# Window attention with transposed scores made from masked keys alone, on one core

## The reference

```python
qkv = x @ in_w.T + in_b
q, k, v = heads of 8 channels
scores = einsum('nhid,nhjd->nhij', q, k) / sqrt(8)
attn = softmax(scores)
out = einsum('nhij,nhjd->nhid', attn, v) @ out_w.T + out_b
y = x + window_reverse(out @ proj_w.T + proj_b)
result = y + fc2(gelu(fc1(ln(y))))
```

## Time and profile before

| | |
|---|---|
| median of 3 runs | 88.28 us (87.34 to 88.77) |
| the profiled execution: span, first to last instruction | 86.4 us |
| around the span, to the median | 1.88 us |
| TensorE busy, matmul records | 79.8 us, 1578 |
| VectorE busy | 66.7 us |
| ScalarE, GpSimd busy | 51.1, 53.3 us |
| TensorE's granted clock, mean | 0.996 of full |

### The profile page before, as it was taken

The page is one execution under the profiler, slowest core; times in us unless marked ns, Lnnn a source line. Parts: engine busy times, 40 slices in busy tenths (PEclk is TensorE's granted clock), DMA queues, the critical chain, the costliest instruction groups (busy, mean ns, idle before and its releaser), DMA issues.

```text
span 86.4 us, 3871 instructions
## 1 busy us (share of the span) xinstructions
PE 79.8 (92%) x1578; PEld 46.1 (53%) x1578; DVE 66.7 (77%) x216; ACT 51.1 (59%) x85; POOL 53.3 (62%) x64
## 2 busy tenths in 40 slices
PE   5999999987999999899999989999999999999950
PEld 5988657444666665664666635554554423223420
DVE  4998998989989979989989987999762964333160
ACT  0296798976358836858578366354588556634400
POOL 7988828995593980899696596896908044800000
PEclk9999999999999999999999999999999999999998
DMA  0999510111010111111111202000000000031142
GB/s 19 206 337 441 231 38 0 34 61 52 31 52 31 46 53 49 53 46 38 46 52 39 66 17 67 31 8 0 8 0 0 0 8 0 0 121 68 53 156 91
DMA packets 3617, 5.72 MB, mean 66 GB/s; under 512 B 1072, under 2 KB 1840, under 8 KB 3472
## 3 DMA queue, kind: packets, MB, share of 16 engines
q1 hardware_dynamic: 2736, 3.08, 11.0%
q10 hardware_dynamic: 864, 2.40, 7.4%
HBM read 2.66 MB, written 1.05 MB: 43 GB/s over the span
## 4 chain that ended last, share of the span: by engine, by line
PE 66%; DVE 21%; issue 8%; ACT 1%; DVEq 0%; ACTq 0%
PE ps_s L323 12%; PE ps_u L414 8%; PE ps_t L275 6%; PE ps_u L484 5%; DVE row_max L644 4%; DVE stats L624 3%; PE ps_t L323 3%; PE ps_t L468 3%; PE ps_t L397 3%; PE ps_m L323 3%; PE ps_s L468 2%; PE ps_m L297 2%; PE ps_o L428 2%; PE ps_o L484 2%; DVE sums L663 2%
## 5 line engine op out<-in xcount | busy, mean ns | idle before, releaser
L1047 POOL TENSOR_TENSOR max_x<-max_t,early 128x512 bf16<-128x512 bf16 x14 | 14.7, 1047 | 9.7 <-DVE max_t L657 9.7
L644 DVE TENSOR_REDUCE row_max<-ps_s 128x16 f32<-128x1024 f32 x15 | 18.1, 1209 | 1.5 <-PE ps_s L323 1.2
L919 ACT ACTIVATE probs<-ps_t 128x1024 f32<-128x1024 f32 x13 | 13.3, 1024 | 8.9 <-PE ps_t L397 8.4
L323 PE MATMUL ps_s<-masked,qk 32*64 32x256 f32 x240 | 16.6, 387 | 1.6 <-DVE row_max L644 0.6
L323 PE MATMUL ps_t<-masked,qk 32*64 32x256 f32 x224 | 15.3, 387 | 0.0
L1056 POOL TENSOR_TENSOR rstd<-y_var,minus_half 128x4 f32<-128x4 f32 x8 | 8.3, 1034 | 6.9 <-DVE y_var L707 6.9
L323 PEld LDWEIGHTS ps_s<-masked,qk 32*64 32x64 f32 x240 | 7.9, 131 | 6.1 <-issue 2.4
L414 PE MATMUL ps_u<-probs,vz 128*32 128x64 f32 x512 | 10.6, 222 | 0.0
L414 PEld LDWEIGHTS ps_u<-probs,vz 128*32 128x32 f32 x512 | 8.0, 109 | 3.4 <-issue 3.0
L1032 POOL TENSOR_TENSOR rstd<-var,minus_half 128x4 f32<-128x4 f32 x8 | 8.6, 1076 | 1.0 <-DVE var L632 0.4
L275 PE MATMUL ps_t<-zeros 128*128 128x128 f32 x32 | 7.1, 389 | 1.0 <-DVE zeros L818 1.0
(11 more groups left out here) (114 smaller groups left out, 149.9 us busy)
## 6 DMA issues: line engine op xcount, KB each, us to landing
masked<-qk SPq DMA_DIRECT2D x54, 32.0 KB, 1.9
x_ch<-x_ch_d ACTq DMA_DIRECT2D x1, 1024.0 KB, 8.1
out_d<-result SPq DMA_DIRECT2D x3, 256.0 KB, 2.5
x_tok<-x_tok_d ACTq DMA_DIRECT2D x1, 512.0 KB, 6.1
late<-late_d ACTq DMA_DIRECT2D x1, 352.0 KB, 5.3
x_tok<-x_tok_d SPq DMA_DIRECT2D x2, 128.0 KB, 3.4
x_tok<-x_tok_d ACTq DMA_DIRECT2D x1, 256.0 KB, 4.9
out_d<-result SPq DMA_DIRECT2D x2, 128.0 KB, 2.3
```

Source lines behind the costliest of these rows:

```text
L323: return nc.tensor.matmul(ps[o:o + L, g, n * TOK:(n + 1) * TOK], qk[r:r + RG, b, w, t], masked[r:r + RG, b, :, w, t], start=(n == 0), stop ...
L644: nc.vector.tensor_reduce(row_max[:, w, 0:16], score_bank(k, w)[:].rearrange("q g (h j) -> q (g h) j", j=L), axis=AX.X, op=ALU.max).then_i ...
L919: nc.scalar.activation(probs[:, w, :], scores_t_bank(k, w)[:].rearrange("q g c -> q (g c)"), ACT.Exp).then_inc(probs_done, 1)
L1047: nc.gpsimd.tensor_tensor(max_x[:, k % 2, w, :].rearrange("q (n i) -> q n i", n=16), bf16_high(max_t[:, w, :]).unsqueeze(1).to_broadcast([ ...
```

## The change

The masked queries are gone. Masked keys serve both products: as moving operand of the straight scores, as before, and as stationary operand of the transposed ones, with the plain queries of one window moving. A stationary operand has 64 columns, one head of one window, so each transposed product of 256 columns becomes four of 64. In each tile both products now use the same rows of the array. So that the straight scores of tile `t+1` and the transposed ones of tile `t` still use different rows, tiles alternate: in even tiles queries (and masked keys) lie on partitions 0 to 63, in odd ones on 64 to 127. The mask buffers are halved, two tiles to a buffer. The bias and the query scale need a second column with the halves swapped, hence two more products and one more VectorE operation at the start. ScalarE's `mask_q_first`, VectorE's `mask_k_half(2)`, the memsets `zero_masked(2)` and `zero_masked(3)`, and 28 of 54 transfers go.

```diff
@@ addresses
+        def q_rows(k):
+            return C * (k % 2)
+        def k_rows(k):
+            return C - q_rows(k)
+        def masked_keys(k, h, w):
+            return masked[q_rows(k):q_rows(k) + C, k // 2 % 2, h, w]
@@ SyncE
-            mask_heads(0, C, 0, q_masked[0], 2)
             for k in range(1, TILES):
-                mask_heads(k, 0, C, k_masked[k % QB], 2 if k in (1, 2) else SLOTS)
-                mask_heads(k, C, 0, q_masked[k % QB])
+                mask_keys(k, 2 if k == 1 else SLOTS)
@@ TensorE
+            def score_t_unit(j, w, n, h, g, u):
+                r = q_rows(j) + RG * g
+                t = slice((2 * n + u) * L, (2 * n + u + 1) * L)
+                c = n * TOK + h * L
+                return nc.tensor.matmul(scores_t_bank(j, w)[L * u:L * u + L, g, c:c + L],
+                                        masked[r:r + RG, j // 2 % 2, h, w, t], qk[r:r + RG, j % QB, w, t],
+                                        start=(n == 0 and h == 0), stop=True,
+                                        skip_group_check=True, tile_position=(r, L * u))
...
             def scores_t_ready(k, w):
-                if w == 0:
-                    pe.wait_ge(q_masked[k % QB], 64 * (k // QB) + (64 if k % QB else 32))
-                if k == 0:
-                    pe.wait_ge(q_masked_act, w + 1)
...
+            def scores_t_block(j, w, n):
+                for h in range(SLOTS):
+                    for g in range(2):
+                        for u in range(2):
+                            score_t_unit(j, w, n, h, g, u)
             def scores_both(k, w, j, v):
...
                 for n in range(BLK):
                     for g in range(2):
                         for u in range(2):
-                            ins = score_unit(ps_s, 0, qk, k, w, n, g, u)
+                            ins = score_unit(k, w, n, g, u)
                     if n == BLK - 1:
                         ins.then_inc(scores_done, 1)
-                    for g in range(2):
-                        for u in range(2):
-                            score_unit(scores_t_bank(j, v), C, qk, j, v, n, g, u)
+                    scores_t_block(j, v, n)
...
+            nc.tensor.matmul(ps_o[0:C, 0, 1:2], w_in_t[0:C, C:2 * C], vec[0:C, B1:B1 + 1],
+                             start=True, stop=True)
+            nc.tensor.matmul(ps_o[C:P, 0, 1:2], w_in_t[0:C, 0:C], vec[0:C, B1:B1 + 1],
                              start=True, stop=True).then_inc(bias_product_done, 1)
@@ VectorE
-                if t == 0:
-                    mask_k_half(2)
...
+            for e in range(2):
+                nc.vector.tensor_scalar(b_qk[:, e:e + 1], ps_o[:, 0, e:e + 1], vec[:, BQK + e:BQK + e + 1],
+                                        vec[:, QS + e:QS + e + 1], op0=ALU.add, op1=ALU.mult).then_inc(b_qk_made, 1)
@@ ScalarE
-            mask_q_first(0)
             copy_xn(1)
-            mask_q_first(1)
@@ GpSimd
-            zero_masked(2)
...
-            pool.wait_ge(max_found, 1)
-            zero_masked(3)
```

More of the change, by code:

```diff
@@ L34 @@
 AHEAD = 3
[L35 to L36 removed]
+NV = 12
+B1, BQK, QS, BV, OUTB, PROJB, B2, FC2B, FC1B = 0, 1, 3, 5, 6, 7, 8, 9, 10
 E_VEC = 0
@@ L103, in swin_block_kernel @@
         qk = sb("qk", [P, QB, 2, TOK])
-        masked = sb("masked", [P, QB, SLOTS, 2, TOK])
+        masked = sb("masked", [P, QB // 2, SLOTS, 2, TOK])
         vz = sb("vz", [P, VB, 2, BLK, HEADS, 4 * D])
@@ L140, in swin_block_kernel @@
         mean_w_set = sem("mean_w_set")
-        masked_zeroed = [sem(f"masked_zeroed{i}") for i in range(QB)]
+        masked_zeroed = [sem(f"masked_zeroed{i}") for i in range(QB // 2)]
         vz_zeroed = sem("vz_zeroed")
@@ L247, in _, with mask_keys @@
         def _(sp):
-            def mask_heads(k, dst, src, done, heads=SLOTS):
-                b = k % QB
+            def mask_keys(k, heads=SLOTS):
                 sp.wait_ge(qk_copied, k + 1)
                 if k < QB:
-                    sp.wait_ge(masked_zeroed[k], 1)
+                    sp.wait_ge(masked_zeroed[k // 2], 1)
                 else:
@@ L316, in project_qkv, with score_unit @@
                 project_v(k)
-            def score_unit(ps, base, stationary, k, w, n, g, u):
-                b = k % QB
-                r = base + RG * g
+            def score_unit(k, w, n, g, u):
+                r = q_rows(k) + RG * g
                 t = slice((2 * n + u) * L, (2 * n + u + 1) * L)
-                o = L * (u if base else u ^ g)
-                return nc.tensor.matmul(ps[o:o + L, g, n * TOK:(n + 1) * TOK], qk[r:r + RG, b, w, t],
-                                        masked[r:r + RG, b, :, w, t], start=(n == 0), stop=True,
+                o = L * (u ^ g)
+                return nc.tensor.matmul(score_bank(k, w)[o:o + L, g, n * TOK:(n + 1) * TOK], qk[r:r + RG, k % QB, w, t],
+                                        masked[r:r + RG, k // 2 % 2, :, w, t], start=(n == 0), stop=True,
                                         skip_group_check=True, tile_position=(r, o))
+            def score_t_unit(j, w, n, h, g, u):
[6 more added lines that the diff above has]
+                                        skip_group_check=True, tile_position=(r, L * u))
             def scores_ready(k, w):
@@ L377, in scores_t @@
                 for n in range(BLK):
-                    for g in range(2):
-                        for u in range(2):
-                            score_unit(scores_t_bank(j, w), C, qk, j, w, n, g, u)
+                    scores_t_block(j, w, n)
             def shift_scores(k, w):
@@ L934, in mask_k_first @@
                 for w in range(2):
-                    nc.scalar.activation(masked[0:C, 0, 3, w], qk[C:P, 0, w], ACT.Copy,
+                    nc.scalar.activation(masked_keys(0, 3, w), qk[C:P, 0, w], ACT.Copy,
                                          scale=slot_mask[C:P, 3:4]).then_inc(k_masked_act, 1)
[L938 to L941, removed]
             def square_mean(k):
```

36 lines of the change are left out of this document (19 added, 17 removed).

## The result

The changed kernel takes **101.19 us** (median of four runs, 100.88 to 102.42) against 88.44: ratio 1.148, 95% interval 1.138 to 1.158. The forecast was 93.5, with a range up to 97.0. The direction was right, the size was not: +12.7 us instead of +5.2. The profiled execution has a span of 99.4 us, 13.0 more than before. Some executions of a kernel take a few per cent longer than others; from here on the time of an experiment is the median of its runs within 1.5% of the fastest, ratios go by these runs, and brackets hold the least and the greatest of all runs.

The account below looks back on a forecast made before the run. It took TensorE to bound the kernel nearly all the way from 21.04 us, VectorE before. Blocks 5.04, a wait taken up -0.3, lone transposed blocks +0.1 and start +0.4 gave 5.2 on 88.28: 93.5 us, range 88.8 to 97.

Parts of the forecast that it names:

- rival 3: TensorE's instruction queue: added instructions come too slowly, with stops per added packet; +2.7 us on the forecast, 96.2; chance 0.10.
- The mixed block: Straight and transposed scores together on TensorE: +0.42 us a block over 1.05, twelve blocks paying, 5.04 us.
- reach: TensorE in mixed blocks: looks 16 products ahead, counted from the oldest unfinished; by the working 0.46 us more a block.
- the second straight group: Sign in the mixed block: its records start near 0.66 us after the block and not at 0.48.
- The start, +0.4: Second bias column before the first mask: 0.2 us on TensorE and 0.2 on VectorE, with 0 and 0.6 as ends.
- The first masks on VectorE: Sign at the start: first masks at about 10.3 us, against 9.87 before, would confirm the start's price.
- the first mixed block: Tile 1's straight scores with tile 0's transposed ones, before 21.04 us with VectorE as the bound: costs nothing.
- What is removed, 0: Query masks, a VectorE mask half, memsets and transfers dropped: 0 gained, at most 1.6 us if their cover were gone.
- no tile's masks come later: Mask transfers: tile 2's two new ones stand where tile 1's query transfers stood, so no delay.
- Rival 1: Mixed blocks: the halves run freely, 0.06 us more a block, 1.2 us in all, 89.5; chance 0.24.
- Rival 4: Masks and transfers: their relief counts and all 1.6 us come back, 87.9 or 86.7; chance 0.08.
- Rival 2: Mixed blocks: strict order or no overlap, or halves taking turns by group at 0.76 a block, 97.6; chance 0.08.

Follow-up runs that it names:

- experiment 7: Kernel before, with products that nothing reads added behind its last one, in parts of 64, 128 and 256 columns; the first part took 11.9 us.
- experiment 5: Changed kernel with its straight score products in one bf16 pass; 96.99 us, ratio to before 1.100.
- experiment 2: Changed kernel with mixed blocks reordered: two heads of transposed products, four straight, three heads, four straight, three heads; 100.03 us, ratio to before 1.145.
- (3, one run): Changed kernel with all 8 straight products of a mixed block ahead of all 32 transposed ones; 99.81 us.
- (6): Changed kernel with its transposed score products in one bf16 pass, all 32 of a block kept; 89.1 us, ratio 1.013.
- experiment 9: Kernel before with the straight score products alone in one bf16 pass; four runs gave 88.02 to 93.04 us.

## Why the prediction was wrong

The step that failed is the delivery of instructions: the sum has no term for it, and rival 3, which stood for it, priced it at +2.7 us. The runs put most of the 12.7 us there. The parts follow one by one.

**The mixed block: the mechanism right, the size too small.** The changed kernel shows the hole: 33 records (16.5 products) are started, then none for 0.2 us until the first straight group is done. Reordering moved the block to 1.33 and to 1.86 as a reach of that size would. The Trainium skill, page "TensorE: Matmul & The Clock Gate", gives a queue of 64 instructions with partial reordering in the table at its head; 33 records with their loads, 66 instructions, agree. I predicted +0.42 (0.46 by the working); it was +0.63. The other 0.17 lies behind the holes: transposed records there start every 16.5 ns and not every 14.6, the fourth head's come before the second straight group (0.73 in place of 0.66), and the last head's take 0.15 in place of 0.06.

**"Instructions come too slowly": the step that failed.** It stood as rival 3 with a chance of 0.10 and +2.7 us. It held two errors. First the price: I took the 0.29 us of idle time for the cost of a stop. But that block of the kernel before took 1.97 us where its neighbours took 1.05, so the stop cost 0.92: behind it, what otherwise stands side by side went one after the other. Second the form: I counted stops per added packet, "one stop in 12 pieces", as if each were a matter of luck. It is a rate. From one stop's end to the next's, where 250 to 256 loads and products lie between them, no profile has less than 3.4 us, and the kernel before went at 4.5 in this stretch, with about a fifth in hand. The change adds 962 instructions to 1,572 there. By an estimate with experiment 7's 3.45 us for 256, the 2,534 need 34.1 us where 27.6 were taken: 6.5 us more in this stretch alone, from the counts, before any block is looked at. Measured were 9.7 more. The price per 256 was not on record before these runs; what the trace did show was the one stop, and that its block took 0.92 us longer.

The Trainium skill, page "Runtime: NRT & Kernel Launch", section "Instruction fetch mechanics", says that instructions come in blocks of 256 and that TensorE has room for 2,048. Experiment 7's 256 between two stops agrees with the first. A store of 2,048 that is used up before the first stop does not show: in the changed kernel the packets come one by one, 3.4 to 5.0 us apart, from 14 to 77 us, and experiment 5's first stop behind 22 us comes after 945 records. Why the changed kernel's first stop comes only at 40 us stays open. The page also holds that the fetch is hidden, because no engine issues faster than about 20 cycles an instruction; here the measurement decides: in tile 0's lone transposed block (15.91 to 17.00 us of the changed kernel) the records start 14.6 ns apart with a load to each, 7.3 ns an instruction, and the stops are the fetch no longer hidden.

**So the sum's terms don't add.** Blocks (+8.0) and stops (+5) look like two causes in the trace. Taking 7 us out of the blocks brought back 4.2, and this one had a packet of instructions fewer (experiment 5), 4.2 brought back 1.2 (2), lengthening them by 2 cost nothing (3, one run). With the instructions taken out, all but 1.1 of the 12.7 came back (6). From about 40 us on the block's length is covered by the delivery, and my whole argument on the reach prices something that is mostly hidden there.

**The start, +0.4:** the trace said +1.2, but the part that belongs to the change is 0.14 at the first scores; the rest differs from execution to execution. The first masks on VectorE, expected at 10.3 us, came at 10.7 in the changed kernel's profile and at 9.6 in experiment 2's. At the lone straight block (21.04 before, 22.24 after) two profiles with early fast steps, experiments 7 and 3, have 20.66 and 21.12. By this one pair 0.4 was about right, though its parts were not: the first mixed block, priced at nothing, lies in it.

**What is removed, 0:** as predicted, as far as these runs tell. Splitting alone, with all masks and transfers kept, took 99.67 (to 102.17) against 101.19; at one pass the changed kernel was not faster than the one before. The transfers are not always free: in experiment 7's profile, whose first 83 us are the kernel before, TensorE waited 1.3 us at 53.97 us for a mask transfer that took 3.6. And one clause was wrong: "no tile's masks come later". All four of tile 2's masks are now transfers; the last landed at 24.70 us in the changed kernel, just ahead of the block at 24.84, and in kernel 2, whose start was faster, TensorE waited 0.5 us for it (the row has also 0.3 us for tile 1's):
```profile
PE ps_t L336 <- DMA masked<-qk: 0.8, 2, 0.5
```

**The rivals.** Rival 1 (halves run freely, 0.24) fell with the first block: 0.73 and not 0.48. Rival 4 needed it. Rival 2's time of 97.6 was nearest to the measurement, but for a reason that is not there: nearness by luck. The right cause, rival 3, had a chance of 0.10 and a price a fifth of the loss.

## What to carry to other kernels

Count instructions before products: an fp32 product is two loads and two passes, and cutting 256 columns into four times 64 quadruples them at equal work. Divide each stage's instructions on the busiest queue by its time; in this kernel 256 in 4.5 us was nearly free (one stop) and 256 in 3.6 to 3.9 us was the wall, and at the wall shorter blocks gave back a fraction of what they saved. Price a stop by how much longer its surroundings take, not by its idle time.

## What the runs showed of the hardware

- TensorE's instructions arrived at no more than 256 in 3.45 us in a stream without waits or transfers (one interval, granted clock mostly 0.50), and 256 in 3.6 to 3.9 us in the attention stage at full clock. The shortest time from one stop's end to the next's in any profile was 3.38 us.
- They came in packets of 16 KB. 72 stops without a releaser ended 1.1 to 1.6 us after a packet had landed; in the changed kernel the next packet started 1.1 to 1.3 us after the stop's end.
- TensorE started instructions out of order up to 16.5 fp32 products ahead of an unfinished one (33 records of products in a block of the changed kernel).
- The moment at which 128-column warm-up products went from 213 to 110 ns differed between executions. In profiles with clock entries, these began there, at full clock, 3.9 to 10.4 us after the first instruction, with no tie to the edits here; the first scores came between 10.4 and 12.4 us with it. A mean granted clock of 1.00 for the time before is not a measurement, since no entry covers it.
- The granted clock fell to 0.50 at times: at 89.6 us in experiment 7, 0.8 us after a stop of 1.18 us in a dense stream, and from 13.8 to 27.4 us in the profile of experiment 9.
